# A fused four-layer network: exponentials with their sum and the normalised result on ScalarE, norm weights in the copy of the transposes

## The reference

```python
out = _layernorm(out + ff, ln3_g, ln3_b)          # over 128 features, times g plus b
```

```python
text_proj  = text_feat @ Wt.T + bt
vision     = mean(vision_feat) @ Wv.T + bv                  # one vector per group
agreement  = sum(text_proj * vision, axis=-1)               # one number per token
routing    = softmax(2 * agreement, over the group's tokens)
gate       = sigmoid(text_proj @ Wg_t.T + (routing * vision) @ Wg_v.T + bg)
fused      = text_feat + gate * routing * vision
out        = (fused - mean) / sqrt(var + eps) * gamma + beta
```

## Time and profile before

| | us |
|---|---|
| median of 3 runs | 2005.97 |
| the profiled execution | 2001.38 |
| its span on the profiler | 1999.8 |
| the edited phase, first token norm to the next phase's first (1198.70 to 1325.67) | 126.97 |
| a full step of it, mean of steps 2 to 5 | 13.67 |

### The profile page before, as it was taken

One profiled execution on the slowest core, in us unless ns is written; L12 is line 12 of the kernel. 1 busy time (PEld: TensorE's weight loads), 2 busy tenths in 40 slices (PEclk: granted clock), 3 DMA queues, 4 the chain that ended last, 5 costly groups with the idle time before them and its releaser, 6 DMA issues. The chain is left out here.

```text
span 1999.8 us, 55013 instructions
## 1 busy us (share of the span) xinstructions
PE 1634.3 (82%) x17114; PEld 1295.9 (65%) x17114; DVE 1369.9 (69%) x4364; ACT 1171.9 (59%) x3299; POOL 942.3 (47%) x1373
## 2 busy tenths in 40 slices
PE   6999889898899677999999775449999885449882
PEld 6888778787787565777777562237777664337671
DVE  3778667676687556888777546868888774427673
ACT  2776657575666335777877432238888773127771
POOL 2354353334443345555666342444454444646773
PEclk8999999999999897999999796769999996559996
DMA  8766666565566003221000000000000000136765
GB/s 229 151 154 133 138 135 130 125 145 127 126 137 142 11 24 123 103 102 67 22 18 16 1 0 0 0 4 1 0 7 14 12 10 16 47 99 207 205 212 158
DMA packets 214845, 167.40 MB, mean 84 GB/s; under 512 B 27632, under 2 KB 188784, under 8 KB 214448
## 3 DMA queue, kind: packets, MB, share of 16 engines
q1 hardware_dynamic: 206128, 142.88, 28.6%
q0 software_dynamic: 8576, 22.88, 3.5%
HBM read 91.92 MB, written 73.76 MB: 83 GB/s over the span
## 5 line engine op out<-in xcount | busy, mean ns | idle before, releaser
L731 ACT ACTIVATE sb_probs<-sb_probs,sb_work 128x128 f32<-128x128 f32 x512 | 198.7, 406 | 168.0 <-DVE sb_work L636 168.0
L281 POOL TENSOR_SCALAR sb_next_var_eps<-sb_next_moments 128x1 f32<-128x1 f32 (+1 forms) x184 | 45.1, 245 | 468.0 <-DVE sb_next_moments L276 467.8
L883 POOL TENSOR_TENSOR sb_work<-sb_work,sb_cols 128x512 f32<-128x512 f32 x128 | 134.2, 1048 | 216.1 <-ACT sb_work L1100 134.5
L1026 DVE TENSOR_REDUCE sb_work<-PS 128x8 f32<-128x512 f32 x256 | 175.3, 685 | 46.2 <-PE PS L925 44.3
L1028 DVE TENSOR_TENSOR sb_work<-PS,sb_work 128x512 f32<-128x512 f32 x256 | 177.1, 692 | 8.8
L1060 ACT ACTIVATE sb_work<-sb_work 128x512 f32<-128x512 f32 x256 | 161.5, 631 | 32.9 <-DVE sb_work L1028 26.8
L899 PE MATMUL PS<-sb_ident,sb_work 128*128 128x128 f32 x1024 | 149.6, 286 | 15.4 <-ACT sb_work L1100 10.1
L952 PEld LDWEIGHTS PS<-sb_v_ones,sb_work 128*64 128x64 f32 x4096 | 132.2, 139 | 24.0 <-issue 15.5
L952 PE MATMUL PS<-sb_v_ones,sb_work 128*64 128x18 f32 x4096 | 144.1, 213 | 4.4 <-ACT sb_work L1066 3.0
L1066 ACT ACTIVATE sb_work<-PS 128x512 f32<-128x512 f32 x256 | 139.5, 595 | 9.3 <-PE PS L899 6.0
L899 PEld LDWEIGHTS PS<-sb_ident,sb_work 128*128 128x128 f32 x1024 | 113.4, 144 | 43.2 <-issue 31.2
(11 more groups left out here) (274 smaller groups left out, 4445.6 us busy)
## 6 DMA issues: line engine op xcount, KB each, us to landing
rel_scratch<-sb_work SPq DMA_DIRECT2D x64, 516.0 KB, 7.7
sb_work<-rel_scratch SPq DMA_DIRECT2D x64, 512.0 KB, 6.5
expert_rows<-sb_blank SPq DMA_DIRECT2D x36, 520.0 KB, 2.9
sb_w_up<-expert_halves SPq DMA_DIRECT2D x23, 512.0 KB, 3.8
sb_w_down<-expert_halves SPq DMA_DIRECT2D x23, 512.0 KB
expert_halves<-sb_e_halves POOLq DMA_DIRECT2D x16, 512.0 KB, 6.1
sb_work<-expert_rows SPq DMA_DIRECT2D x23, 260.0 KB, 3.3
sb_e_raw<-e_W POOLq DMA_DIRECT2D x16, 256.0 KB, 5.8
```

The lines of the kernel that those rows point to most:

```text
L731: ins = e.activation(probs[:, j], probs[:, j], ACT.Exp, bias=neg_max[:, j:j + 1], scale=-1.0, accum_out=row_sum[:, j:j + 1])
L883: e.tensor_tensor(k_masked[:, u3], k_sb[:, u3].rearrange("p (b k) -> p b k", b=2).unsqueeze(2) .to_broadcast([P, 2, 4, S]), col("place").u ...
L1026: e.tensor_reduce(top, mine, AX.X, ALU.max).then_inc(sem("att_max_ready"), 1)
```

## The change

In the l2 phase:
- The maximum of each batch is multiplied by -2 (eight columns). ScalarE takes the exponential straight from PSUM, one instruction per batch with this shift as its bias and the sum of the batch as its accumulator output. The subtraction (L1424) and the sum (L1383) are gone.
- The stage's norm: GpSimd makes -mean, and behind the power -mean * inv_std. ScalarE then makes x * inv_std - mean * inv_std out of PSUM for each of four tiles. VectorE multiplies all four tiles by gamma in one instruction and adds beta in another. L1406 and L1430 are gone.
- The tokens' norm: VectorE makes only (x - mean) * inv_std; the weights g and b, now kept by feature (one column each), are the scale and bias of ScalarE's copy of the transposes.
- TensorE's sum over features waits for the exponentials of the unit before instead of for the subtraction.

```diff
 l2_pool, step:
                 if late:
                     wait_alone(e, sem("l2_f_moments"), n)
+                    e.tensor_scalar(f_minus_mean, f_moments[:, :, 0], -1.0, None, ALU.mult)
                     e.tensor_scalar(f_var_eps, f_moments[:, :, 1], EPS, None, ALU.add).then_inc(sem("l2_f_var_eps"), 1)
...
                 if late:
                     wait_alone(e, sem("l2_f_var_eps"), n)
+                    wait_alone(e, sem("l2_f_scaled"), n - 1)
                     e.tensor_tensor(f_inv_std, f_var_eps, half_power[:, :], ALU.pow).then_inc(sem("l2_f_inv_std"), 1)
+                    wait_alone(e, sem("l2_f_inv_std"), 2 * n - 1)
+                    e.tensor_tensor(f_shift, f_minus_mean, f_inv_std, ALU.mult).then_inc(sem("l2_f_inv_std"), 1)
 l2_tensor, step:
-                    wait(e, sem("l2_agree_shifted"), m)
+                    wait(e, sem("l2_exp_done"), m)
                     e.matmul(PS[:, 2], ones, tv.rearrange("p b s -> p (b s)"), start=True, stop=True)\
 l2_vector, step:
-                if back:
-                    e.wait_ge(sem("l2_exp_done"), n + 1)
-                    wait(e, sem("l2_inv_ready"), n)
-                    e.tensor_reduce(l2_sum, routes[:, u], AX.X, ALU.add).then_inc(sem("l2_sum_ready"), 1)
...
                 if back:
-                    e.wait_ge(sem("l2_sum_ready"), n + 1)
+                    e.wait_ge(sem("l2_exp_done"), n + 1)
                     wait(e, sem("l2_sums_used"), n)
                     e.reciprocal(l2_inv, l2_sum).then_inc(sem("l2_inv_ready"), 1)
...
-                if late:
-                    e.wait_ge(sem("l2_f_moments"), n)
-                    wait(e, sem("l2_out_ready"), n - 1)
-                    for t in range(QT):
-                        ins = e.scalar_tensor_tensor(f_scaled[:, t], PS[:, 4 + 3 * v, P * t:P * t + P],
-                                                     f_moments[:, t, 0:1], row("l2_g"), ALU.subtract, ALU.mult)
-                    ins.then_inc(sem("l2_f_scaled"), 1)
...
                     e.tensor_reduce(l2_max, by_batch(PS[:, 2]), AX.X, ALU.max).then_inc(sem("l2_max_ready"), 1)
                     e.wait_ge(sem("l2_max_ready"), m + 1)
-                    e.tensor_tensor(routes[:, v], by_batch(PS[:, 2]), over_tokens(l2_max), ALU.subtract)\
-                        .then_inc(sem("l2_agree_shifted"), 1)
+                    wait(e, sem("l2_exp_done"), m)
+                    e.tensor_scalar(l2_shift, l2_max, -2.0, None, ALU.mult).then_inc(sem("l2_shift_ready"), 1)
                 if late:
+                    quad = X[:, bass.ds(QT * (n - 1), QT)]
                     e.wait_ge(sem("l2_f_scaled"), n)
-                    e.wait_ge(sem("l2_f_inv_std"), n)
-                    for t in range(QT):
-                        ins = e.scalar_tensor_tensor(X[:, bass.ds(QT * (n - 1) + t, 1)].rearrange("p a d -> p (a d)"),
-                                                     f_scaled[:, t], f_inv_std[:, t:t + 1], row("l2_b"),
-                                                     ALU.mult, ALU.add)
-                    ins.then_inc(sem("l2_out_ready"), 1)
+                    wait_alone(e, sem("l2_out_ready"), n - 1)
+                    e.tensor_tensor(f_scaled, f_normed, row("l2_g").unsqueeze(1).to_broadcast([P, QT, D]), ALU.mult)\
+                        .then_inc(sem("l2_out_scaled"), 1)
+                    wait_alone(e, sem("l2_out_scaled"), n)
+                    e.tensor_tensor(quad, f_scaled, row("l2_b").unsqueeze(1).to_broadcast([P, QT, D]), ALU.add)\
+                        .then_inc(sem("l2_out_ready"), 1)
...
                 if head:
-                    quad_norm_vector(e, LQ * NQ, k, u, ("ln13_g", "ln13_b"), False, None)
+                    quad_norm_vector(e, LQ * NQ, k, u, None, False, None)
 l2_scalar, step:
+                if late:
+                    e.wait_ge(sem("l2_f_inv_std"), 2 * n)
+                    wait_alone(e, sem("l2_out_scaled"), n - 1)
+                    for t in range(QT):
+                        ins = e.activation(f_normed[:, t], PS[:, 4 + 3 * v, P * t:P * t + P], ACT.Identity,
+                                           bias=f_shift[:, t:t + 1], scale=f_inv_std[:, t:t + 1])
+                    ins.then_inc(sem("l2_f_scaled"), 1)
                 if back:
                     e.wait_ge(sem("l2_gate_summed"), n + 1)
                     e.activation(gate, gate, ACT.Tanh, scale=0.5, bias=half_bg).then_inc(sem("l2_gate_tanh"), 1)
                 if front:
-                    e.wait_ge(sem("l2_agree_shifted"), m + 1)
-                    e.activation(routes[:, v], routes[:, v], ACT.Exp, scale=2.0).then_inc(sem("l2_exp_done"), 1)
+                    e.wait_ge(sem("l2_shift_ready"), m + 1)
+                    wait(e, sem("l2_gate_summed"), m - 1)
+                    wait(e, sem("l2_wv_ready"), m - 1)
+                    for b in range(NBU):
+                        ins = e.activation(routes[:, v, b], PS[:, 2, S * b:S * b + S], ACT.Exp, bias=l2_shift[:, b:b + 1],
+                                           scale=2.0, accum_out=l2_sum[:, b:b + 1])
+                    ins.then_inc(sem("l2_exp_done"), 1)
                 if head:
-                    quad_keep_scalar(e, LQ * NQ, k, u, split=False)
+                    quad_keep_scalar(e, LQ * NQ, k, u, gb=("ln13_gc", "ln13_bc"), split=False)
```

More of the change, by code:

```diff
@@ L55 @@
                   ("sa_bq", 1), ("sa_bk", 1), ("ca_bq", 1), ("ca_bk", 1),
-                  ("sa_bv", 1), ("ca_bv", 1), ("ln11_gc", 1), ("ln11_bc", 1),
+                  ("sa_bv", 1), ("ca_bv", 1), ("ln11_gc", 1), ("ln11_bc", 1), ("ln13_gc", 1), ("ln13_bc", 1),
                   ("group", 4), ("place", 4)):
@@ L64 @@
 ROWS = ("ln01_g", "ln01_b", "l0_b2", "ln02_g", "ln02_b", "msa_bo", "ln11_g", "ln11_b", "ca1_bo", "ln12_g",
-        "ln12_b", "l1_b2", "ln13_g", "ln13_b", "l2_g", "l2_b", "sa_bo", "ca_bo", "misc", "plan")
+        "ln12_b", "l1_b2", "l2_g", "l2_b", "sa_bo", "ca_bo", "misc", "plan")
 def wait(e, sem, value):
@@ L1290, in build @@
         l2_max = carve((NBU,))
+        l2_shift = carve((NBU,))
         l2_sum = carve((NBU,))
@@ L1298, in build @@
         f_inv_std = carve((QT,))
+        f_shift = carve((QT,))
+        f_minus_mean = carve((QT,))
         f_scaled = carve((QT, D))
+        f_normed = carve((QT, D))
         LQ = 2
@@ L1379, in step @@
                     ins.then_inc(sem("l2_f_stats"), 1)
-                if back:
-                    e.wait_ge(sem("l2_exp_done"), n + 1)
-                    wait(e, sem("l2_inv_ready"), n)
-                    e.tensor_reduce(l2_sum, routes[:, u], AX.X, ALU.add).then_inc(sem("l2_sum_ready"), 1)
                 if late:
                     wait_alone(e, sem("l2_f_stats"), n)
-                    wait_alone(e, sem("l2_f_inv_std"), n - 1)
-                    wait_alone(e, sem("l2_f_scaled"), n - 1)
+                    wait_alone(e, sem("l2_f_inv_std"), 2 * n - 2)
                     for t in range(QT):
@@ L1418, in step @@
                     e.wait_ge(sem("l2_agree_done"), m + 1)
-                    wait(e, sem("l2_agree_shifted"), m)
                     e.tensor_reduce(l2_max, by_batch(PS[:, 2]), AX.X, ALU.max).then_inc(sem("l2_max_ready"), 1)
                     e.wait_ge(sem("l2_max_ready"), m + 1)
-                    wait(e, sem("l2_gate_summed"), m - 1)
-                    wait(e, sem("l2_wv_ready"), m - 1)
-                    e.tensor_tensor(routes[:, v], by_batch(PS[:, 2]), over_tokens(l2_max), ALU.subtract)\
-                        .then_inc(sem("l2_agree_shifted"), 1)
+                    wait(e, sem("l2_exp_done"), m)
+                    e.tensor_scalar(l2_shift, l2_max, -2.0, None, ALU.mult).then_inc(sem("l2_shift_ready"), 1)
                 if late:
+                    quad = X[:, bass.ds(QT * (n - 1), QT)]
                     e.wait_ge(sem("l2_f_scaled"), n)
-                    e.wait_ge(sem("l2_f_inv_std"), n)
-                    for t in range(QT):
-                        ins = e.scalar_tensor_tensor(X[:, bass.ds(QT * (n - 1) + t, 1)].rearrange("p a d -> p (a d)"),
-                                                     f_scaled[:, t], f_inv_std[:, t:t + 1], row("l2_b"),
-                                                     ALU.mult, ALU.add)
-                    ins.then_inc(sem("l2_out_ready"), 1)
+                    wait_alone(e, sem("l2_out_ready"), n - 1)
[4 more added lines that the diff above has]
+                        .then_inc(sem("l2_out_ready"), 1)
                 if back:
@@ L1952, in lay_out @@
             "sa_bv": L3["sa_in_b"][2 * D:], "ca_bv": L3["ca_in_b"][2 * D:],
-            "ln11_gc": L1["ln1_g"], "ln11_bc": L1["ln1_b"], "group": group, "place": place}
+            "ln11_gc": L1["ln1_g"], "ln11_bc": L1["ln1_b"],
+            "ln13_gc": L1["ln3_g"], "ln13_bc": L1["ln3_b"], "group": group, "place": place}
     T["cols"] = c(np.concatenate([vals[n].reshape(P, -1) for n in COLS], axis=1))
@@ L1966, in lay_out @@
```

(2 more changed lines are left out.)

## The result

The changed kernel takes 2013.86 us (median of 7 runs, 2009.44 to 2018.21) against 2005.45 for the kernel before (7 runs, 2000.79 to 2006.39). The ratio is 1.0049, 95% interval 1.0033 to 1.0064: 8.4 us slower. Forecast were 2013.5 us and +7.5.

The account below looks back on a forecast made before the run. A chain of waits through all engines, not VectorE's 89% busy time, was taken as the bound. Terms of -3.5, +3.9 and +7.1 made +7.5 us on 2005.97: 2013.5 us, 8-in-10 range 2004 to 2020.

Parts of the forecast that it names:

- first three steps: Start of the l2 phase, without the stage's norm: saved VectorE time is on the path, -3.5 us.
- step 1: First full step of the l2 phase, lower TensorE clock: 14.83 us against 14.81, so 0.
- steps 2 to 5: Four full steps of the l2 phase, each 0.97 us longer: +3.9 us.
- step 6: Late l2 step without tokens' norm: gated product starts at about +9.8 instead of +7.50, +2.3 us.
- step 7: Late l2 step: gated product starts at +8.19 instead of +5.87, +2.3 us.
- The norms on ScalarE: Stage's norm in a full step: four tiles take 1.49 us (1.0 to 1.81), ending at +8.16.
- The two products: VectorE's gamma and beta passes over 512 columns: 1.50 us instead of L1430's 1.14.
- The tokens' norm stays stretched: VectorE's four operations keep 2.14 us beside GpSimd's fused sum; rival: unstretched at 1.11 us, 2007.3 us in all, chance 0.17.
- The exponentials: Eight on ScalarE take 2.6 us, hidden with 2.2 us of cover before the copy; rival: exposed, 2019 us, chance 0.04.
- The rival in which they are held: GpSimd's small operations slowed while VectorE reads two SBUF tensors: +0.47 us in eight steps, 2017 us, chance 0.15.
- The clock: TensorE's clock shifts: 2008 us at 2.4 GHz throughout, 2015 at 1.2 GHz (+0.3 in four steps); chance 0.06.
- the ring: Chain of waits through all engines from one l2 projection to the next: 13.56 us becomes 14.53, +0.97 per full step.

Follow-up runs that it names:

- e6: Kernel before with tokens' norm and exponentials parts, tokens' norm moved ahead on VectorE's queue, right behind the shift: phase 112.80 us, ratio 0.9925.
- e7: Changed kernel with each exponential made twice, the extra eight into a tile nothing reads: phase 139.14 us, ratio 1.0074.
- e5: Changed kernel with the tokens' norm moved ahead on VectorE's queue, right behind the shift: phase 126.63 us, ratio 1.0003.
- e1: Kernel before with the tokens' norm part alone: phase 123.10 us, ratio 0.9972.
- e4: Changed kernel with the stage's norm undone, leaving the tokens' norm and exponentials parts: phase 121.31 us, ratio 0.9956.
- e3: Changed kernel with its tokens' norm part undone, leaving the exponentials and stage's norm parts: phase 145.41 us, ratio 1.0086.
- e2: Kernel before with the exponentials part alone: phase 126.60 us, ratio 0.9988.

## Why the prediction was right

The mechanism and the size were right. Point by point, for the phase:

| part | forecast | measured |
|---|---|---|
| first three steps | -3.5 | -4.2 |
| step 1 | 0 | +0.1 |
| steps 2 to 5 | +3.9 | +5.3 |
| step 6 | +2.3 | +2.9 |
| step 7 | +2.3 | +2.3 |
| step 8 | +2.5 | +2.7 |
| together | +7.5 | +8.95 |

- *The norms on ScalarE.* 1.49 us forecast, 1.51 measured; the shift ready at +6.52 and +6.74; the norms' end at +8.16 and +8.37.
- *The two products.* 1.50 us forecast, 1.59 measured: between them lie 0.21 us, and not the 0.12 that stood behind L1146.
- *The tokens' norm stays stretched.* 2.06 us for four, where the first two steps, without a fused sum, took 1.11, and so did e6. GpSimd's fused sum starts 0.17 us behind the group; the second of the four instructions started 0.09 us after it and took 1.29 us, until 0.08 us behind the sum's end. The Trainium skill states such a rule in "SBUF — State Buffer", section "SBUF: two separate sides", for the port pair that VectorE and GpSimd share: it is an exclusive lock for a whole instruction, and whoever comes second is blocked. The trace agrees: the group is 0.95 us longer. The page says it of a VectorE operation in a two-port mode or with two SBUF inputs; whether this one is of these no run here shows.
- *The exponentials.* 2.6 us forecast, 2.48 measured (1278.57 to 1281.05), hidden. e7 shows the cover.
- *GpSimd's small operations* took 0.25 and 0.23 us. The rival in which they are held came true once, in step 7, where one of them took 0.71; in the other seven steps it did not.
- *The clock.* The term that I had mis-sized: I took the mixed clock of before as given and gave 0.06 to all shifts of TensorE's clock together, with +0.3 us in each of four steps for the lower level. It fell from 0.75 to 0.61 in steps 2 to 5. In the changed kernel that costs mostly a longer projection: the three steps at 2.07 us took 15.08 us on average, the one at 1.82 us 14.71 us. So 1.1 of the 5.3 us are the clock's, near the 1.2 of that rival, and step 5's remaining +1.1 against the earlier trace rows is the ring's (0.97 forecast). In step 6 the clock fell too, from 0.82 to 0.63. There it explains at most 0.2 of the 0.6 us that were missing: e5 has the same work in step 6 and took 13.43 us in it at 0.75, against 13.60.
- *The second strand.* The ring that I drew ran through GpSimd's power alone. In the changed kernel that did no harm, since ScalarE's norms made the strand through the power the longer one by far. In e1 and e4 it made my forecasts too good.

That the total came out at 2013.86 against 2013.5 is in part luck: the phase cost 1.45 us more than forecast, the median of the kernel before was 0.5 us lower when more runs were in it, and the rest of the program varies by more than that.

What the change is made of, then: its tokens' norm part is worth -9.5 us (changed kernel against e3), its stage's norm part costs 14.6 (against e4) to 18.8 (e2 to e3), and its exponentials part is worth 0.4 us on the kernel before (e2) and 1.8 on e1 (e1 to e4). No run takes the exponentials part out of the changed kernel itself.

## What to carry to other kernels

Where every engine's queue is written out by hand, first follow one period of the loop from an instruction back to its own next copy: only what lies on that ring has a price, and an engine that is busy for 89% can have a part beside it. Look for a second strand that ends nearly as late (0.23 us here): it takes over as soon as the first is shortened, or as soon as it slows down. Moving work from a full engine to an idle one costs the hand-overs too, and whatever is queued behind the wait. When a move leaves the full engine waiting, look for work in its queue that needs nothing of the wait and put it ahead: that one move was worth 9.3 us here on the changed kernel and 8.5 on e4.

## What the hardware showed that I had not expected

- TensorE's granted clock in one phase was the same to 0.01 in two profiles of each of two kernels, and small edits on other engines change it: 0.75 before and in e2, 0.61 in the changed kernel, 0.57 to 0.71 in the others. With 1.1 us of VectorE's work taken out of a step (e1) it was 0.62 instead of 0.75, and the phase gained 3.9 us where 9 were expected.
- What a lower clock costs depends on what lies on the ring: 1.28 us per step in e6, nothing that can be seen in e5.
- A loop can fall into a pattern in which its steps take the two levels in turn (e6: 12.64 and 11.36 us). A mean over steps hides this.
